# Second phase of the feed-forward in 17 tiles of 256 rows in place of 9 tiles of 512

## The reference

```python
winners = jnp.argmax(bids, axis=-1)                       # one of 3 experts for each token
hr = jnp.square(jax.nn.relu(jnp.einsum('nc,ech->enh', flat_h, K_rwkv)))    # experts 0 and 1: 256 -> 1024
out_rwkv = jnp.einsum('enh,ehc->enc', hr, V_rwkv)                          # 1024 -> 256
out_trans = flat_h @ W1 * jax.nn.sigmoid(flat_state @ W2) @ W3             # expert 2
final = jnp.einsum('ne,enc->nc', onehot, all_out) * scale
return x + final.reshape(B, T, C)
```

## Time and profile before

| | |
|---|---|
| median of 3 runs | 2665.5 us (2656.21 to 2667.6) |
| the profiled execution | 2670.99 us, its span from first to last instruction 2669.2 us |
| second phase, run 0 (rows asked for to last matmul) | 1376.4 to about 1595 us |
| second phase, run 1 | 2437.6 to about 2656 us, the program ends at 2669.2 us |
| TensorE busy over the span | 2247.3 us (84%) |
| VectorE, ScalarE, GpSimd busy | 1565.0, 1013.9, 759.2 us |
| mean granted TensorE clock | 0.928 of full speed |

### The profile page before, as it was taken

The page is one execution under the profiler, slowest core; times in us unless marked ns, Lnnn a source line. Parts: engine busy times, 40 slices in busy tenths (PEclk is TensorE's granted clock), DMA queues, the critical chain, the costliest instruction groups (busy, mean ns, idle before and its releaser), DMA issues. The chain is left out here.

```text
span 2669.2 us, 49971 instructions
## 1 busy us (share of the span) xinstructions
PE 2247.3 (84%) x18702; PEld 1776.6 (67%) x18702; DVE 1565.0 (59%) x3407; ACT 1013.9 (38%) x1828; POOL 759.2 (28%) x816
## 2 busy tenths in 40 slices
PE   4469999999999999699859993788888876895998
PEld 2357888788877888577749981445444445774997
DVE  7965547464554646378745653655555526874664
ACT  0223333333333333243424441345454553342553
POOL 4360101010110101136622233333333204662222
PEclk9779999999999999889979996899999998997999
DMA  4320000000000000212345536544444407112553
GB/s 148 99 68 10 10 9 17 2 17 10 9 10 9 11 8 2 78 56 80 127 151 141 140 57 149 91 73 73 74 73 73 73 27 230 40 44 64 139 143 56
DMA packets 152489, 179.60 MB, mean 67 GB/s; under 512 B 48761, under 2 KB 138769, under 8 KB 149137
## 3 DMA queue, kind: packets, MB, share of 16 engines
q1 hardware_dynamic: 137884, 155.67, 21.9%
q0 software_dynamic: 13440, 17.90, 4.1%
q10 hardware_dynamic: 944, 2.88, 0.4%
HBM read 107.66 MB, written 68.75 MB: 66 GB/s over the span
## 5 line engine op out<-in xcount | busy, mean ns | idle before, releaser
L2249 DVE TENSOR_REDUCE b_neg_max<-bank 128x1 f32<-128x512 f32 (+2 forms) x384 | 178.7, 506 | 184.4 <-PE bank L2477 182.1
L2369 ACT ACTIVATE b_probsT<-bank 128x512 f32<-128x512 f32 x320 | 185.9, 604 | 209.8 <-PE bank L2477 198.5
L2008 PE MATMUL bank<-e_hT_hi,k_rwkv 128*128 128x512 f32 x576 | 206.9, 401 | 2.9 <-DVE e_hT_lo L1912 2.9
L1933 DVE TENSOR_TENSOR e_square<-e_relu 128x512 f32<-128x512 f32 x144 | 99.7, 693 | 148.5 <-ACT e_relu L1972 146.1
L774 POOL TENSOR_TENSOR probs<-probs,rcp 128x512 f32<-128x512 f32 x64 | 66.7, 1044 | 382.8 <-DVE rcp L642 382.8
L1972 ACT ACTIVATE e_relu<-bank,k_bias 128x512 f32<-128x512 f32 x144 | 99.1, 688 | 199.4 <-PE bank L2008 199.2
L2021 PE MATMUL bank<-v_rwkv_hi,e_hidden_lo 128*128 (+1 forms) x576 | 162.5, 282 | 0.0
L2021 PE MATMUL bank<-v_rwkv_lo,e_hidden_hi 128*128 (+1 forms) x576 | 162.1, 282 | 0.0
L2021 PE MATMUL bank<-v_rwkv_hi,e_hidden_hi 128*128 (+1 forms) x576 | 161.8, 281 | 0.0
L621 DVE TENSOR_TENSOR conv_lo<-bank,conv_hi 128x512 fp32r<-128x512 f32 x64 | 44.2, 691 | 141.9 <-ACT conv_hi L791 141.9
L2477 PE MATMUL bank<-b_k_stacked,b_q_stacked 96*128 96x512 bf16 (+3 forms) x512 | 126.4, 309 | 0.0
(11 more groups left out here) (358 smaller groups left out, 6431.9 us busy)
## 6 DMA issues: line engine op xcount, KB each, us to landing
k_rwkv<-scratch_k SPq DMA_DIRECT2D x16, 2048.0 KB, 7.4
scratch_b_parts<-b_part SPq DMA_DIRECT2D x96, 128.0 KB, 1.8
b_q_stacked<-scratch_b_parts SPq DMA_DIRECT2D x96, 128.0 KB, 4.5
b_k_stacked<-scratch_b_parts SPq DMA_DIRECT2D x96, 128.0 KB, 4.4
scratch_rows<-f_hq SPq DMA_DIRECT2D x18, 516.0 KB, 8.6
e_rows<-scratch_rows SPq DMA_DIRECT2D x18, 516.0 KB, 8.4
x_tokens<-in_x_dram SPq DMA_DIRECT2D x8, 512.0 KB, 7.7
scratch_x_out<-x_tokens SPq DMA_DIRECT2D x8, 512.0 KB, 3.0
```

Of the source, the lines that this page charges most:

```text
L1933: nc.vector.tensor_tensor(sq[:, q % 2], r[:, q % 2], r[:, q % 2], ALU.mult).then_inc(s["square_done"], 1)
L2008: last = nc.tensor.matmul(data[:], ff.k_part(i % 2, a)[:, k, c * P:(c + 1) * P], hT[b][:, i % 2, k], start=n == 0, stop=n == len(steps) - 1)
L2249: last = nc.vector.tensor_reduce(neg_max[:, half % 2, t, head + e:head + e + 1], data[:, at:at + (t + 1) * P], AX_X, ALU.max, negate=True)
L2369: nc.scalar.activation(probsT[:, ring, u], fl.data("st", pair, u)[:], ACT.Exp, scale=DB ** -0.5).then_inc(fl.released("st", pair, u), 1)
```

## The change

A tile becomes 256 rows (RT = 2 groups of 128), so 4096 positions and one tile more are 17 tiles. A bank now holds two chunks of the inner layer side by side, 256 columns each: q = 4 i + c with QT = 4 such pairs in a tile. `hidden(q)` is 12 matmuls of 256 columns, `second(q)` 12 of 256 columns as before (2 chunks x 2 row groups x 3 products). Relu is two instructions of 256 columns, since each chunk has its own bias, with a semaphore behind both; the square and its two parts stay 512 columns wide. The two halves of the transposed rows share one bank, and so do the two row groups of the result. `deliver` moves from c = 1 to c = 0, `turned_hi` and `turned_lo` from c = 4 to c = 2, `take` from c = 5 to c = 2, and `turn` from c = 2 to c = 1. The rows cleared at the start of the feed-forward are the 4352 that there are now.

```diff
-TILES = B + 1
-POSITIONS = TILES * T
+RT = 2
+ROWS = RT * P
+TILES = B * T // ROWS + 1
+POSITIONS = TILES * ROWS
+CLEARS = -(-POSITIONS // T)
+QT = HT // 2
...
-            order += [(("e", i, b), 2 + 2 * (i % 2) + b) for b in range(2)]
-        if c == 2 and i + 1 < TILES:
-            order += [(("hT", i + 1, k), 6 + k) for k in range(CT)]
+            order += [(("e", i), 2 + i % 2)]
+        if c == 1 and i + 1 < TILES:
+            order += [(("hT", i + 1), 6 + (i + 1) % 2)]
...
             def load_k(i):
                 which = sp.value_load(ff.flags[0:1, sequence[i]:sequence[i] + 1], min_val=0, max_val=1)
-                sp.wait_ge(*read("h", (i - 1) * HT - 1))
+                sp.wait_ge(*read("h", (i - 1) * QT - 1))
                 sp.dma_start(ff.kbuf[i % 2][:].bitcast(F32), moe.k[bass.ds(which, 1)].rearrange("e p n -> (e p) n")).then_inc(k_loaded[i % 2], 16)
...
             def turned_lo(i):
-                for k in range(CT):
-                    ready((s["hT_hi"], i * CT + k + 1))
-                    nc.vector.tensor_tensor(hT[1][:, i % 2, k], fl.data("hT", i, k)[:], hT[0][:, i % 2, k].bitcast(F32),
-                                            ALU.subtract).then_inc(fl.released("hT", i, k), 1)
+                ready((s["hT_hi"], i + 1))
+                nc.vector.tensor_tensor(flat(hT[1][:, i % 2]), fl.data("hT", i)[:], flat(hT[0][:, i % 2]).bitcast(F32), ALU.subtract).then_inc(
+                    fl.released("hT", i), 1)
 
             def deliver(i):
-                ready((s["taken"], 2 * (i + 1)))
+                ready((s["taken"], 2 * (i + 1)), full("e", i))
                 if i >= 2:
                     ready(added(i % 2, i // 2))
-                for t in range(TT):
-                    ready(full("e", i, t // 2))
-                    nc.vector.tensor_scalar(y[:, i % 2, t, :], fl.data("e", i, t // 2)[:, t % 2 * C:(t % 2 + 1) * C], scale[:, i % 3, t:t + 1],
-                                            None, ALU.mult).then_inc(s["y_done"], 1)
-                    if t % 2:
-                        ready((s["y_done"], i * TT + t + 1))
-                        dve.sem_inc(fl.released("e", i, t // 2), 1)
+                for t in range(RT):
+                    nc.vector.tensor_scalar(y[:, i % 2, t, :], fl.data("e", i)[:, t * C:(t + 1) * C], scale[:, i % 3, t:t + 1], None,
+                                            ALU.mult).then_inc(s["y_done"], 1)
+                ready((s["y_done"], (i + 1) * RT))
+                dve.sem_inc(fl.released("e", i), 1)
...
+                i, c = divmod(q, QT)
+                ready((s["relu_done"], 2 * (q + 1)))
+                nc.vector.tensor_tensor(flat(sq[:, q % 2]), flat(r[:, q % 2]), flat(r[:, q % 2]), ALU.mult).then_inc(s["square_done"], 1)
                 ready((s["square_hi"], q + 1), (s["square_done"], q + 1))
-                nc.vector.tensor_tensor(h2[1][:, q % SQ_RING], sq[:, q % 2], h2[0][:, q % SQ_RING].bitcast(F32), ALU.subtract).then_inc(
-                    s["hidden_done"], 1)
-                if c == 1 and i:
+                nc.vector.tensor_tensor(flat(h2[1][:, q % SQ_RING]), flat(sq[:, q % 2]), flat(h2[0][:, q % SQ_RING]).bitcast(F32),
+                                        ALU.subtract).then_inc(s["hidden_done"], 1)
+                if c == 0 and i:
                     deliver(i - 1)
-                if c == 4 and i + 1 < TILES:
+                if c == 2 and i + 1 < TILES:
                     turned_lo(i + 1)
-                if c == 5 and i + 2 < TILES:
+                if c == 2 and i + 2 < TILES:
...
             def turned_hi(i):
-                for k in range(CT):
-                    act.wait_ge(*full("hT", i, k))
-                    nc.scalar.activation(hT[0][:, i % 2, k], fl.data("hT", i, k)[:], ACT.Copy).then_inc(s["hT_hi"], 1)
+                act.wait_ge(*full("hT", i))
+                nc.scalar.activation(flat(hT[0][:, i % 2]), fl.data("hT", i)[:], ACT.Copy).then_inc(s["hT_hi"], 1)
 
             def hidden(q):
-                i, c = q // HT, q % HT
+                i, c = divmod(q, QT)
                 if q >= 2:
                     act.wait_ge(s["square_done"], q - 1)
                 if c == 0 and i >= 2:
                     act.wait_ge(k_loaded[i % 2], 32 * (i // 2))
                 act.wait_ge(*full("h", q))
-                nc.scalar.activation(r[:, q % 2], fl.data("h", q)[:], ACT.Relu, bias=ff.k_bias[i % 2][:, c:c + 1]).then_inc(
-                    fl.released("h", q), 1)
-                act.wait_ge(*read("h", q))
-                nc.scalar.activation(h2[0][:, q % SQ_RING], r[:, q % 2], ACT.Square).then_inc(s["square_hi"], 1)
+                for n in range(2):
+                    nc.scalar.activation(r[:, q % 2, n], fl.data("h", q)[:, n * ROWS:(n + 1) * ROWS], ACT.Relu,
+                                         bias=ff.k_bias[i % 2][:, 2 * c + n:2 * c + n + 1]).then_inc(s["relu_done"], 1)
+                act.wait_ge(s["relu_done"], 2 * (q + 1))
+                act.sem_inc(fl.released("h", q), 1)
+                nc.scalar.activation(flat(h2[0][:, q % SQ_RING]), flat(r[:, q % 2]), ACT.Square).then_inc(s["square_hi"], 1)
 
             turned_hi(0)
             for q in range(N):
                 hidden(q)
-                if q % HT == 4 and q // HT + 1 < TILES:
-                    turned_hi(q // HT + 1)
+                if q % QT == 2 and q // QT + 1 < TILES:
+                    turned_hi(q // QT + 1)
...
             def turn(i):
                 pe.wait_ge(rows_loaded[i % 2], 16 * (i // 2 + 1))
+                data = begin("hT", i)
                 for k in range(CT):
-                    data = begin("hT", i, k)
-                    for t in range(TT):
-                        last = nc.tensor.transpose(data[:, t * P:(t + 1) * P], rows[:, i % 2, t, k * P:(k + 1) * P], core.ident[:])
-                    last.then_inc(fl.filled("hT", i, k), 1)
+                    for t in range(RT):
+                        last = nc.tensor.transpose(data[:, k * ROWS + t * P:k * ROWS + (t + 1) * P], rows[:, i % 2, t, k * P:(k + 1) * P],
+                                                   core.ident[:])
+                last.then_inc(fl.filled("hT", i), 1)
             def hidden(q):
-                i, c = q // HT, q % HT
+                i, c = divmod(q, QT)
+                if c == 0 and i >= 2:
+                    pe.wait_ge(k_loaded[i % 2], 32 * (i // 2))
                 if c == 0:
-                    for k in range(CT):
-                        pe.wait_ge(*read("hT", i, k))
-                    if i >= 2:
-                        pe.wait_ge(k_loaded[i % 2], 32 * (i // 2))
+                    pe.wait_ge(*read("hT", i))
                 data = begin("h", q)
-                for n, (k, a, b) in enumerate(steps):
-                    last = nc.tensor.matmul(data[:], ff.k_part(i % 2, a)[:, k, c * P:(c + 1) * P], hT[b][:, i % 2, k], start=n == 0,
-                                            stop=n == len(steps) - 1)
+                for half in range(2):
+                    for n, (k, a, b) in enumerate(steps):
+                        at = (2 * c + half) * P
+                        last = nc.tensor.matmul(data[:, half * ROWS:(half + 1) * ROWS], ff.k_part(i % 2, a)[:, k, at:at + P], hT[b][:, i % 2, k], start=n == 0,
+                                                stop=n == len(steps) - 1)
                 last.then_inc(fl.filled("h", q), 1)
...
+                for half in range(2):
+                    chunk = 2 * c + half
+                    values = [w[:, bass.ds(expert, 1), chunk, :].rearrange("p e c -> p (e c)") for w in ff.v]
+                    for t in range(RT):
+                        for n, (a, b) in enumerate(PASSES):
+                            last = nc.tensor.matmul(fl.data("e", i)[:, t * C:(t + 1) * C], h2[a][:, q % SQ_RING, half, t * P:(t + 1) * P],
+                                                    values[b], start=chunk == 0 and n == 0 and t == 0, stop=chunk == HT - 1 and n == 2,
+                                                    skip_group_check=True)
+                if c == QT - 1:
+                    last.then_inc(fl.filled("e", i), 1)
...
                 second(q, expert)
-                if c == 2 and i + 1 < TILES:
+                if c == 1 and i + 1 < TILES:
                     turn(i + 1)
```

More of the change, by code:

```diff
@@ L1300, in _ @@
             sp.wait_ge(s["empty_done"], 2)
-            for i in range(TILES):
-                sp.dma_start(moe.rows[i * T:(i + 1) * T, :].rearrange("(t p) c -> p t c", p=P), empty).then_inc(rows_cleared, 16)
+            for i in range(CLEARS):
+                tiles = min(TT, (POSITIONS - i * T) // P)
+                sp.dma_start(moe.rows[i * T:i * T + tiles * P, :].rearrange("(t p) c -> p t c", p=P), empty[:, 0:tiles]).then_inc(rows_cleared, 16)
             if prepares:
@@ L1516, in _ @@
                     if j == 1:
-                        ready((rows_cleared, TILES * 16))
+                        ready((rows_cleared, CLEARS * 16))
```

(37 more changed lines are left out.)

16 lines of the change are left out of this document (6 added, 10 removed).

## The result

| | before | after |
|---|---|---|
| median (lowest to highest, runs) | 2665.5 us (2656.21 to 2672.66, 7) | 2683.91 us (2678.58 to 2687.06, 7) |
| profiled execution, its span | 2670.99, 2669.2 us | 2684.44, 2682.6 us |
| second phase of run 1, rows asked for to last matmul's start | 218.4 us | 232.2 us |
| the same of run 0 | 218.4 us | 231.9 us |
| from there to the end of the program | 13.2 us | 10.0 us |

The change makes the kernel slower: ratio 1.0072, 95% interval 1.0051 to 1.0093, 18 us. The forecast was 2692, in a range of 2677 to 2714. The four phase rows give +13.8 - 3.2 in run 1 and +13.5 - 3.8 in run 0, +20.3 us together. That agrees with the 18 us of the medians, whose interval is 14 to 25 us.

What follows compares the result with a forecast made beforehand. TensorE's list was taken to bound the kernel. Per run -9.2 (matmuls) + 27.2 (turns) - 4.8 (head and tail) = +13.2 us, twice +26.4, on 2665.5 gives 2692 us; range for 8 in 10: 2677 to 2714.

Steps and rivals of the forecast that it cites:

- The pause: TensorE, first `hidden` behind a tile's transposes: waits for copy and subtraction, 1.46 us idle, 34 waits in all.
- A turn: TensorE, between tiles: 2.14 us each, 16 times a run, 34.2 us against 7.0, so 27.2 us more.
- The matmuls: TensorE, second phase: a pair of chunks at 2.84 us, 68 a run, 9.2 us less per run.
- the lower bound: TensorE, twelve narrow `hidden` matmuls: 1.39 us for the same columns, making it 11.3 us less per run.
- Head and tail: Start and end of the second phase: shorter first load, first turn and final adds, together 4.8 us less a run.
- The relu: ScalarE: two of 256 columns at 470 ns each for one of 512, 0.25 us more latency per pair.
- `deliver`: VectorE: comes a chunk early and idles for the tile's last `second`, up to 2 us, harmlessly.
- the rival at 2712 to 2746: TensorE's clock falls behind the pauses: +20 us at 12 of 32 pauses, +54 us at all; chance 13%.
- The adds and the weights: Shared DMA engines: forecast in time; rival that they come late, 1.9 us for each of 30 tiles, 2749 us, chance 5%.

Runs made afterwards that it cites:

- run 1: Not an experiment: the later of the two feed-forward runs inside one kernel execution; its second phase takes 218.4 us before the change, 232.2 us after.
- run 0: Not an experiment: the earlier of the two feed-forward runs inside one kernel execution; its second phase takes 218.4 us before the change, 231.9 us after.
- the high parts first: Changed kernel, first `hidden` of a tile does its 8 high-part products before waiting for the low part: 2667.18 us, ratio 0.999.
- the early turn: Changed kernel with turn(i + 1) behind pair c = 0 in place of c = 1: 2632.9 us, ratio 0.9849.
- the last experiment: Against the early turn, `deliver` moved from c = 0 to c = 1 and `take` from c = 2 to c = 3: 2630.74 us, ratio 0.985.
- the small loads: Changed kernel, each load of first-layer weights fetches 64 KB and not 2 MB: 2691.81 us, ratio 1.0077.

## Why the prediction was right, and where its sizes were off

- **The pause.** Forecast 34 waits of 1.46 us; measured 34 of 1.45. A turn was priced at 2.14 us and measures 2.15; from the first transpose to the first `hidden` it is 2472.07 - 2470.01 = 2.06 us, forecast 2.05. Taking the pause away gives 1.66 us a turn back, where the price less the transposes is 1.72; taking 0.73 us of it away, with the high parts first, gives 0.75.
- **The matmuls** are the mis-sized term. I priced a pair of chunks at 2.84 us, by the neighbouring group of twelve, and gave 1.39 per group as the lower bound; the group takes 1.36 and the pair 2.79, below even that bound, 2.81. 68 x 0.05 = 3.4 us a run, 6.8 in all: most of the distance from 2692 to 2683.9. By the phase rows the forecast's +26.4 was +20.3; the last 2 us, down to the 18.4 of the medians, are within their spread. Tiles of run 1 take 13.32 us on average, forecast 13.5. The kernel before with narrow matmuls shows the same by itself.
- **Head and tail.** The first rows landed in 2.74 us against 3.75 (forecast 0.9 less, measured 1.0), and the end comes 3.2 us sooner behind the last matmul (forecast 3.1). From the rows asked for to the first `hidden`, run 1 takes 2445.72 - 2440.42 = 5.30 us against 2444.83 - 2437.60 = 7.23, 1.9 less (forecast 1.75). Half of that is lost again, a term that the forecast did not have: the clock is still at its lower level then. It reaches 1.00 5.6 us behind the first `hidden`, where it took 3.8 before. The first three groups of `hidden`, after and then before, and the window in which the clock rises, after and then before:

```profile
2445.72 6.96 PE bank L2016 x36
```

```profile
2444.83 6.15 PE bank L2008 x18
```

```profile
2450.42:2451.42 1.00, 1.00 (x7) 1.00 (x7) 0.63 (x1) 0.17 (x1) 0.00 (x0) 0.56 0.00 0
```

```profile
2448.60:2449.60 1.00, 1.00 (x5) 0.82 (x5) 0.89 (x2) 0.52 (x1) 0.00 (x0) 1.00 0.00 0
```

Three groups at 1.36 us would be 4.1 us and three at 1.39 4.2, so the lower clock costs 2.9 us after and 2.0 before. The sum for the phase of run 1 up to its last matmul, -12.6 for the pairs at 2.79, +27.4 for the turns, -1.9 for the head and +0.9 for the clock, is +13.8, as measured. In run 0 the same reading gives -2.2 for the head and +0.5 for the clock, +13.1 against +13.5.
- **The relu** of 256 columns takes 471 ns, estimated at 470 from a copy. `deliver` waits for the last `second`, 1.9 us at most; with the early turn, where it waits as long, the last experiment shows that this costs nothing.
- **The clock** stayed at 1.00 behind all pauses of both phases, so the rival at 2712 to 2746 did not come. By the Trainium skill, "TensorE: Matmul & The Clock Gate", section "Why this matters for your kernels", idle gaps between bursts of matmuls send the engine to its lower clock if they are long enough. No gap of 1.46 us did so in this trace; gaps of 2.07 us did at some tiles (last section).
- **The adds and the weights.** In the changed kernel VectorE never waits for a landed add and TensorE never for `k_rwkv`, and the small loads gain nothing. The landing time on the page of the profile deserves a second look: it reads 12.6 us, against 7.4 before, almost the 13.2 us that a load has until it is needed. Yet with the early turn it reads 14.3 us, where a load issued at 2477.40 is needed by the `hidden` at 2489.16, 11.8 us later, and TensorE still waits for no weights. The windows of the changed kernel behind an issue at 2485.56 show where the bytes went:

```profile
2486.00:2488.00 2.00, 2.00 (x20) 2.00 (x19) 0.78 (x2) 0.91 (x3) 0.00 (x0) 1.00 0.79 197
2488.00:2493.00 5.00, 5.00 (x46) 5.00 (x45) 2.87 (x5) 2.39 (x6) 0.86 (x1) 1.00 0.93 378
2493.00:2498.80 5.80, 4.34 (x38) 4.13 (x37) 2.92 (x8) 2.57 (x7) 2.62 (x2) 1.00 0.46 64
```

2 x 197 + 5 x 378 = 2.28 MB by 2493, nearly all of the 2.36 MB of the weights and the rows asked for with them: 7.5 us, about as before. With the early turn at least, the landing time on the page is later than the time from which the weights can be used; what it is read off stays open.

## What to carry to other kernels

Cutting a tile in half can take away more than half of the work that stands between a step and its reader. Here it went from three chunks to nothing. The list runs ahead by AHEAD = 2 entries, and an entry became a pair of chunks, so the reader moved up, to the middle of the tile before; `turn` moved back, from behind three of eight chunks to behind two of four pairs. So count, in the list of the engine that bounds the kernel, what is left between the two, and set the latency of the other engines (here a copy and a subtraction, 1.46 us with the hand-overs) against it. The small tiles themselves are a gain, fewer padded rows and a shorter tail, and the version to keep is the change with its turn one pair earlier: 2632.9 us, 1.5% below the kernel before. If a step cannot move, order the reader's products by what arrives first: that alone took half of the pause.

## What the runs showed of the hardware that I had not expected

- Twelve matmuls of 256 columns with twelve weight loads take 1.36 us, six of 512 columns with six loads 1.39; `second`, at the same width and number, takes 1.42. Why these two groups differ by 0.06 us was not tried.
- The attention stage has seven pauses of 2.07 us, one a tile, and one of 2.35. Behind them the granted clock is lower in some executions at one tile and in others at another. Before, it was so behind the first three of the seven; after, behind the third and fourth, and behind the eighth pause. Here are the windows behind the first and the third of after, to be read beside the earlier trace rows, where the first had 0.67:

```profile
264.34:269.34 5.00, 5.00 (x52) 4.55 (x54) 0.69 (x1) 0.60 (x1) 0.00 (x0) 1.00 0.02 3
...
502.32:507.32 5.00, 5.00 (x35) 4.59 (x36) 0.00 (x0) 0.60 (x1) 0.00 (x0) 0.66 0.01 3
```

The change does not touch that stage, and the same pause is followed by either level. The spread of single executions shows in that stage as a whole, too: counted from pause to pause, a tile of it (the last one left out) takes 116 us where the mean granted clock is 0.99, and 118 to 121 us where it is 0.94 to 0.97. Two neighbours of before:

```profile
382.00:498.00 116.00, 110.34 (x1224) 93.60 (x1224) 63.90 (x130) 42.42 (x82) 12.08 (x12) 0.99 0.04 11
498.00:619.00 121.00, 114.88 (x1224) 97.49 (x1224) 64.08 (x130) 42.53 (x82) 12.09 (x12) 0.94 0.04 10
```

Before has one such tile at 0.99 and after has three, which is most of the 9.7 us by which run 0's phase starts sooner there. That is a reason to compare phases by their own rows.
